# One PSUM bank in place of two for the transposed probabilities, and one for the sums over heads, in an attention block (Trainium2, one core)

## What is computed

```python
h = take(L0_tok_weight, x)
h = h + L0_attn(layernorm(h))          # linear attention, 8 heads of 16
h = h + L0_ffn(layernorm(h))           # 32 experts, each picks its 512 best tokens
h = h + L1_attn(layernorm(h))          # <- here
h = h + L1_ffn(layernorm(h))           # 8 experts, 2 for each token

def L1_attn(x, Wq, Wk, Wv, Wo, bo):    # 64 blocks of 256 tokens, 8 heads of 128
    q, k, v = split_heads(x @ Wq), split_heads(x @ Wk), split_heads(x @ Wv)
    dot = causal(einsum('bhqe,bhke->bhqk', q / sqrt(128), k))
    out = einsum('bhqk,bhke->bhqe', softmax(dot), v)
    return join_heads(out) @ Wo + bo
```

## Time and profile before

| | us |
|---|---|
| median of 3 runs (lowest, highest) | 3125.21 (3123.84, 3127.59) |
| the profiled execution's own time | 3104.09 |
| its span, first to last instruction | 3102.4 |
| PE busy with matmuls, of the span | 2371.3 (76%) |
| DVE busy | 2124.0 (68%) |
| ACT busy | 1286.3 (41%) |
| POOL busy | 1103.1 (36%) |
| granted TensorE clock, mean | 0.867 |

### The profile page before, as it was taken

How to read it: one execution, slowest core, us unless ns; L and a number is a source line. 1 busy time by engine, 2 the same in 40 slices (tenths; PEclk the granted TensorE clock), 3 DMA queues, 4 the chain that set the end, 5 groups by cost and what they waited for, 6 DMA issues and landing times.

```text
span 3102.4 us, 54712 instructions
## 1 busy us (share of the span) xinstructions
PE 2371.3 (76%) x16057; PEld 2091.5 (67%) x16057; DVE 2124.0 (68%) x9114; ACT 1286.3 (41%) x3921; POOL 1103.1 (36%) x1145
## 2 busy tenths in 40 slices
PE   5887841066666599999999999999999757777720
PEld 4776731045555599999999899999999656666620
DVE  4666778854444388889888888889888724444333
ACT  4656620012222355555555555555555323333310
POOL 6444300068888311222212221222212335555520
PEclk9888865577777799999999999999999878889865
DMA  2222210034444400000000000000000022222259
GB/s 82 74 67 69 76 33 0 0 57 77 76 74 74 76 21 22 26 27 27 26 22 28 25 27 23 26 25 29 25 23 28 26 79 75 73 74 76 75 177 276
DMA packets 227432, 170.55 MB, mean 55 GB/s; under 512 B 23773, under 2 KB 213808, under 8 KB 227136
## 3 DMA queue, kind: packets, MB, share of 16 engines
q1 hardware_dynamic: 181568, 105.90, 12.3%
q0 software_dynamic: 45568, 61.15, 8.8%
HBM read 86.96 MB, written 81.04 MB: 54 GB/s over the span
## 4 chain that ended last, share of the span: by engine, by line
PE 54%; DVE 20%; POOL 10%; issue 8%; DMA 3%; DVEq 2%; another core or an unknown queue 2%; SPq 1%; ACT 1%; POOLq 0%; ACTq 0%
PE bank L1889 7%; POOL hbuf L707 6%; PE bank L1949 6%; PE bank L1935 5%; PE bank L1897 5%; DVE junk L1180 5%; PE bank L1909 4%; PE bank L1886 3%; PE bank L1911 3%; PE bank L1910 3%; PE bank L2030 3%; POOL xe L699 3%; PE bank L2019 3%; DMA vo_place<-h3buf 3%
## 5 line engine op out<-in xcount | busy, mean ns | idle before, releaser
L750 POOL DMA_INDIRECT spread_rows<-kb,pos x256 | 249.5, 975 | 731.4 <-ACT pr_place L934 619.9
L778 POOL DMA_INDIRECT zbuf<-vo_place x272 | 271.8, 999 | 227.3 <-DVE vo_place L1634 140.1
L1889 PE MATMUL bank<-xT,gT 128*128 128x256 f32 x1024 | 333.6, 408 | 0.0
L932 ACT ACTIVATE pr_place<-bank,nmax 128x128 f32<-128x128 f32 x512 | 187.9, 367 | 333.8 <-DVE nmax L1359 328.8
L1377 DVE COPY pr_place<-bank 128x384 f32<-128x384 f32 x512 | 280.7, 548 | 0.2 <-issue 0.2
L2019 PE MATMUL bank<-kb,pc 128*128 128x256 f32 x544 | 174.6, 451 | 123.2 <-DVE pc L1614 104.2
L1949 PE MATMUL bank<-wvo_part,x_part 128*128 128x512 f32 x768 | 268.0, 457 | 0.0
L1897 PE MATMUL bank<-ident,pr_place 128*128 128x128 f32 x1536 | 254.5, 275 | 8.9 <-DVE pr_place L1370 8.9
L962 ACT ACTIVATE vo_place<-bank 128x512 f32<-128x512 f32 x256 | 153.1, 598 | 238.6 <-PE bank L1949 237.9
L1897 PEld LDWEIGHTS bank<-ident,pr_place 128*128 128x128 f32 x1536 | 194.0, 140 | 83.8 <-DVE pr_place L1370 30.0
L1935 PE MATMUL bank<-x_part,wqk_part 128*128 128x256 f32 x1536 | 246.0, 296 | 1.2 <-DVE x_part L1484 1.2
(11 more groups left out here) (298 smaller groups left out, 6196.1 us busy)
## 6 DMA issues: line engine op xcount, KB each, us to landing
vo_place<-spread_rows SPq DMA_DIRECT2D x136, 130.0 KB
vo_place<-zbuf SPq DMA_DIRECT2D x32, 512.0 KB, 4.3
xrow<-xr SPq DMA_DIRECT2D x32, 320.0 KB
hbuf<-h SPq DMA_DIRECT2D x32, 256.0 KB
hx<-hbuf SPq DMA_DIRECT2D x64, 128.0 KB, 2.3
h3buf<-h SPq DMA_DIRECT2D x64, 128.0 KB, 1.8
vo_place<-h3buf SPq DMA_DIRECT2D x32, 256.0 KB, 4.6
out_dram<-vo_place SPq DMA_DIRECT2D x32, 256.0 KB, 2.9
```

The source lines that it names most:

```text
L750: pool.indirect_dma_start(out=spread_rows, out_offset=bass.IndirectOffsetOnAxis(ap=pos[:, k, j:j + 1], axis=0), in_=xr4s[g % 2][:, k, j], ...
L778: pool.indirect_dma_start(out=zbuf, out_offset=bass.IndirectOffsetOnAxis(ap=xu[:, q, j, C + 1:XW].bitcast(U32), axis=0), in_=yu[:, q % YR, ...
L1889: pe.matmul(s2[:, P:3 * P], g[:, P:2 * P], xT3[:, p], start=False, stop=True, skip_group_check=True)\
```

## The change

The transposes of all units go to bank 5, the sums of all blocks to bank 1; banks 6 and 7 are no longer used in this stage. What reused a bank after two units now reuses it after one, so two waits ask for one step more: `turns(u)` waits for the copy of unit u-1 (it waited for that of u-2), and the first sum of block n for `finish(n-1)` (it waited for `finish(n-2)`). No instruction is added, removed or moved on any engine, and the SBUF buffers stay as they are.

```diff
-        GBANK, VBANK, SBANK, TBANK, OBANK = 0, 2, (3, 4), (5, 6), (1, 7)
+        GBANK, VBANK, SBANK, TBANK, OBANK = 0, 2, (3, 4), 5, 1
...
-                dve.tensor_copy(prT[:, h % 2], bank[TBANK[h % 2]][:, 0:3 * P]).then_inc(prT_ready, 1)
+                dve.tensor_copy(prT[:, h % 2], bank[TBANK][:, 0:3 * P]).then_inc(prT_ready, 1)
...
-                dve.tensor_tensor(h3[:, q], bank[OBANK[q]][:, 0:2 * P].rearrange("p (j c) -> p j c", j=2), hb[:, q], ALU.add)\
+                dve.tensor_tensor(h3[:, q], bank[OBANK][:, 0:2 * P].rearrange("p (j c) -> p j c", j=2), hb[:, q], ALU.add)\
...
             def turns(u, h):
                 pe.wait_ge(pr_ready, u + 1)
-                if not isinstance(u, int) or u >= 2:
-                    pe.wait_ge(prT_ready, u - 1)
+                if u >= 1:
+                    pe.wait_ge(prT_ready, u)
                 for k in range(3):
-                    ins = pe.transpose(bank[TBANK[h % 2]][:, k * P:(k + 1) * P], pr[:, h % 4, k * P:(k + 1) * P], ident[:])
+                    ins = pe.transpose(bank[TBANK][:, k * P:(k + 1) * P], pr[:, h % 4, k * P:(k + 1) * P], ident[:])
                 ins.then_inc(prT_mm, 1)
 
             def sums(u, h, p, n):
-                o = bank[OBANK[p]]
+                o = bank[OBANK]
                 pe.wait_ge(prT_ready, u + 1)
                 if h == 0:
                     pe.wait_ge(vo_ready, 4 * n + 4)
-                    if not isinstance(n, int) or n >= 2:
-                        pe.wait_ge(h3_ready, n - 1)
+                    if n >= 1:
+                        pe.wait_ge(h3_ready, n)
```

## The result

The changed kernel takes 3148.15 us (median of 5 runs, 3139.59 to 3149.65) against 3125.34 us for the kernel before (5 runs, 3123.84 to 3133.05). The ratio is 1.0061, with a 95% interval of 1.0042 to 1.0079: slower by 0.6%, about 19 us. The ratio goes by the mean of the five runs; the two medians lie further apart, 22.8 us. The forecast was 3140, with a range of 3131 to 3152.

The account below looks back on a forecast made before the run. PE was taken to set the pace in the second attention. Slots 5 to 7 and slot 0, 0.29 + 0.20 = 0.49 us a pair, times 31 pairs = 15.2 us, added to the median gave 3140; range 3131 to 3152.

Parts of the forecast that it names:

- The bank of sums at 0: First sums of each block in the second attention: waiting for the previous block's `finish` costs 0, with 0.63 us to spare.
- No queue changes, the wait is what costs: PE's transposes: nothing is added to any queue; the wait for the previous unit's copy moves ahead of the transposes.
- Slots 5 to 7, paid once: PE waits for the copy in each of these slots, but the delays don't add up: 0.29 us a pair.
- A: Rival, slots 5 to 8: the waits add up, about 1.7 us a pair or 52 us, giving 3177; chance 0.08.
- Slot 0 adds its own: PE's transposes in slot 0 wait for the copy too, making PE 0.20 us late a pair.
- The size of a wait: PE's transposes: release 0.05 us after the copy ends, then 0.39 until the sums; 0.10 saved at sums that had waited.
- Handed on by DVE's wait for scores: From slot 10 and in slots 2 to 4, DVE waits for scores, so PE's delay passes on; some 15 us more.
- The sum over 31 pairs: The second attention: 0.29 + 0.20 = 0.49 us a pair, times 31 pairs = 15.2 us.
- The lower bound: Waiting transposes lose nothing, or sums have nothing to save: about 0.35 us a pair, 11 us.
- C: Rival: PE stands for every copy, 3406, or its clock falls to 0.78, 3516; chance 0.03 for both.
- B: Rival, slots 4 to 7: PE's shift parts `norm_rest` from POOL's add, DVE comes up to 0.47 us earlier, 3125; chance 0.09.
- What would show it: Signs: 44.17 us a pair; transposes' weight loads wait for the copy about 120 times, not for L1370; idle time about doubles.

Follow-up runs that it names:

- e3: The kernel before with one bank for the sums and its later wait, two for the transposes: 43.67 us a pair, ratio 0.999.
- e6: The changed kernel with POOL's add of the residual put off to slots 1 and 9: 44.23 us a pair, ratio 1.0073 to the kernel before.
- e1: The kernel before with both pairs of banks kept; only the transposes wait as in the change: 44.28 us a pair, ratio 1.0055.
- e4: The changed kernel with the two waits ahead of the transposes in the other order: 44.16 us a pair, ratio 1.0056 to the kernel before.
- e7: The kernel before with POOL's add put off to slots 1 and 9, its scatters and copy kept at their places: 43.20 us a pair, ratio 0.9952.
- e5: The kernel before with POOL's add of the residual put off to slots 1 and 9: 43.68 us a pair, ratio 0.9997.
- e9: e7 with the gate's layer norm cut short (no statistics, three steps of the inverse root): 42.69 us a pair, 0.9886 of the kernel before.
- e2: The kernel before with one bank for the transposes and its later wait, two for the sums: 44.28 us a pair, ratio 1.0054.

## Why the prediction was right, point by point

- **The bank of sums at 0**: right. e3 took 43.67 us a pair, and no wait of the sums for `finish` stands in the profile after. It was said that a wait would appear if DVE fell back by more than 0.6 us against PE; in e6 it does.
- **No queue changes, the wait is what costs**: right. e1 has the whole price with two banks.
- **Slots 5 to 7, paid once**: right in kind. Three waits, and 0.35 us behind them; A, by which they add up to 1.7 us a pair, didn't come. DVE's slack of 0.6 us covered the 0.35 as it was said to cover 0.29.
- **Slot 0 adds its own**: right, 0.26 in place of 0.20.
- **The size of a wait, "A release reaches PE 0.05 us after the copy ends"**: this term was mis-sized, and it is the whole miss of 0.11 us a pair. The 0.05 came from sums, whose weight load carries its only wait itself. The transposes have two waits, and the one that ends last is a separate instruction: 0.15 from the copy's end to the first transpose, less the 0.03 to 0.04 that the group itself then loses less. 0.50 in place of 0.44, twice a pair, is 0.12; e4 took it away and came to 0.48.
- **Handed on by DVE's wait for scores**: right. 16.9 us more in the same 195 places, where some 15 had been said.
- **The sum over 31 pairs**: 31 x 0.60 = 18.6 us, and the attention grew by 19.0. The median, 3148, lies 8 us above the forecast. The mis-sized term is 3.4 of these; the rest is how the two medians fell, mostly outside the attention, and the few us that the range left for scatter took it up.
- **The lower bound**: its working is not sound. Sums that have nothing to save make the change dearer, not cheaper: without that saving slot 7 would be 0.39 us late and not 0.29. With transposes that lose nothing, the other half of that bound, it is 0.37 a pair, 11.5 us, so the figure came out nearly the same.
- **The clock**: 1.00 throughout; C didn't come. The Trainium skill's account of a clock that oscillates from small idle times (TensorE: Matmul & The Clock Gate, A second HAM failure mode) is not what this stage shows: some 130 waits of up to 1.5 us, and 1.00 granted. The argument that no new gap would be longer than the longest before didn't hold for the weight loads: 1.5 us against 1.2.
- **B, not slower**: the change didn't bring it, for POOL's add moved with DVE, as was said against it: `norm_rest` still takes 0.82 us in slot 4. That it takes 0.35 elsewhere is too wide a reading: in slots 3, 6 and 8 of the kernel before its median is 0.54, 0.53 and 0.69. But the hold-up it named is worth 0.48 us a pair to whoever removes it (e7).
- **What would show it**: in 131 units the transposes start 0.15 us after the copy's end, where about 120 were said, but the view names L1370 or "issue" for the weight loads' waits. Their idle time rose from 30.0 to 78.6 us, 2.6 times and not twice. The sign "no longer for L1370" would have misled.

## What to carry to other kernels

A second buffer is worth what the reader's lateness is, slot by slot, and not its share of instructions: here only 4 slots of 16 needed it (slot 14 in a few pairs besides), and the second bank of sums was needed in none, until POOL's later work took its room away (e6). Waits in a row of such slots cost once if the engine waited for keeps its own time; find the place where it starts to wait in turn, for there the delay becomes the loop's. Where an instruction has two waits, let it carry the one that ends last (0.06 us each time here). And when work is put off on an in-order queue, look at what stands behind it: e5 took a hold-up of 0.47 us out of slot 4, brought scatters and a copy into slots 9 to 11, where DVE then lost 1.33 us, and gained nothing, while e7 kept the rest in place and gained 0.5%.

## What the runs showed of the hardware

- The place of a wait has a price: 0.05 us from the end of DVE's copy to the weight load that carries the wait (e4), 0.12 when it stands ahead of it as an instruction of 51 ns (changed kernel).
- A weight load that waited gives a slower group (0.38 us from the first transpose to the sums, against 0.35 behind a separate wait and 0.33 without one), so 0.03 of what the better order saves is given back: the transposes start 0.09 us earlier, the sums 0.06.
- A DVE instruction on SBUF that starts just behind an add or copy of POOL can be held until about its end: 0.82 in place of 0.35 us beside the add (L1370, slot 4, ending 0.16 us after it), 0.62 in place of 0.15 beside the copy (L1039 in e5, 0.02 after it).
- A semaphore's event can come well after the end of the product that raises it: 0.86 us for the scores in slot 11 of e5, about 0.95 for the transposes in slot 3 of e5 and e9 (where PE doesn't wait on it), against 0.01 elsewhere. The cause is open, and the ends of PE's rows are modelled.
- Writing transposes into the PSUM bank that DVE has just finished reading costs nothing measurable: e1 (two banks) and e2 (one), 44.28 both.
